# Delta-attention loop on one core: a loop turn takes two sequences (four tiles) instead of one (two tiles)

## The reference, cut to what matters

```
qkvz = x @ W_in                                # x is layer-normalised; 128 -> 4*1024
q, k, v = silu(conv4(q, k, v))                 # causal, 4 taps, per channel
q = l2norm(q) * HD ** -0.5 ; k = l2norm(k)
def step(S, (q, k, v, g, beta)):               # over the 256 tokens of a sequence, S starts at 0
    S = S * exp(g)
    S = S + k (outer) (v - k @ S) * beta
    return S, q @ S
y = y * rsqrt(mean(y*y) + 1e-6) * norm_w * silu(z)
x = x + y @ W_o
```

## Time and profile before

| | |
|---|---|
| median of 3 runs | 7055.97 us |
| lowest, highest | 7048.7, 7073.78 us |
| the profiled execution's own time | 7079.48 us |
| its span, first to last instruction | 7077.4 us |
| mean granted TensorE clock | 0.917 |
| PE busy over the span | 6006.2 us (85%) |
| DVE, ACT, POOL busy over the span | 3698.0, 3271.5, 2513.9 us |

### The profile page before, as it was taken

One profiled execution on the slowest core, in us unless ns is written; L12 is line 12 of the kernel. 1 busy time (PEld: TensorE's weight loads), 2 busy tenths in 40 slices (PEclk: granted clock), 3 DMA queues, 4 the chain that ended last, 5 costly groups with the idle time before them and its releaser, 6 DMA issues. The chain is left out here.

```text
span 7077.4 us, 188914 instructions
## 1 busy us (share of the span) xinstructions
PE 6006.2 (85%) x68003; PEld 4474.9 (63%) x68004; DVE 3698.0 (52%) x7183; ACT 3271.5 (46%) x7090; POOL 2513.9 (36%) x2357
## 2 busy tenths in 40 slices
PE   5999999999999999999999999675888678886587
PEld 4666666666666666666666666463666456665486
DVE  5555554555555554554555554654444456665433
ACT  2555554555555554554555554142333244553165
POOL 5445444444444444444444443342000100002554
PEclk9999998999999998999999999897999889997588
DMA  3000000000000000000000000111000000001124
GB/s 97 16 18 20 20 14 20 18 16 20 20 14 20 18 15 20 14 20 20 14 20 20 20 14 14 37 47 42 0 0 0 2 1 0 0 0 31 37 59 120
DMA packets 99093, 159.13 MB, mean 22 GB/s; under 512 B 19972, under 2 KB 82244, under 8 KB 96068
## 3 DMA queue, kind: packets, MB, share of 16 engines
q1 hardware_dynamic: 76260, 121.44, 5.3%
q0 software_dynamic: 14080, 26.64, 1.1%
q10 hardware_dynamic: 8320, 4.19, 0.2%
HBM read 118.03 MB, written 104.87 MB: 31 GB/s over the span
## 5 line engine op out<-in xcount | busy, mean ns | idle before, releaser
L784 PE MATMUL bank<-wc,hT 128*128 128x512 f32 x2088 | 1156.8, 676 | 120.9 <-issue 107.6
L941 PE MATMUL bank<-X,kqe 128*128 128x64 f32 x6240 | 774.2, 277 | 75.2 <-DVE rb L1426 54.6
L941 PEld LDWEIGHTS bank<-X,kqe 128*128 128x128 f32 x6240 | 726.3, 192 | 99.2 <-DVE rb L1426 70.2
L1171 ACT ACTIVATE TT<-bank 128x512 bf16<-128x512 f32 x640 | 382.1, 597 | 731.7 <-PE bank L922 729.3
L784 PEld LDWEIGHTS bank<-wc,hT 128*128 128x128 f32 x2088 | 393.0, 212 | 448.9 <-issue 425.8
L1465 DVE TENSOR_TENSOR yb<-bank,masks 128x512 bf16<-128x512 f32 x768 | 527.3, 687 | 256.4 <-PE bank L904 248.0
L1405 DVE TENSOR_TENSOR kqe<-bank,ex 128x512 f32<-128x512 f32 x520 | 335.1, 686 | 337.7 <-PE bank L850 337.7
L1301 POOL TENSOR_SCALAR_AFFINE_SELECT kqe<-kqe 128x512 f32<-128x512 f32 x260 | 215.0, 827 | 817.2 <-DVE kqe L1405 817.2
L1268 POOL TENSOR_TENSOR qa<-qa,qt 128x512 f32<-128x512 f32 x390 | 486.3, 1268 | 34.8 <-POOL qt L1263 34.8
L1171 ACT ACTIVATE T<-bank 128x512 bf16<-128x512 f32 x640 | 348.9, 595 | 272.6 <-PE bank L915 270.6
L1126 ACT ACTIVATE ex<-bank,gate_bias_all 128x128 f32<-128x128 f32 x1040 | 290.0, 372 | 384.6 <-DVE kqe L1405 183.6
(11 more groups left out here) (526 smaller groups left out, 13338.5 us busy)
## 6 DMA issues: line engine op xcount, KB each, us to landing
sent_l0f<-blank_l0f SPq DMA_DIRECT2D x64, 528.0 KB
sent_l1m<-blank_l1m SPq DMA_DIRECT2D x64, 528.0 KB
xin<-sent_l1m SPq DMA_DIRECT2D x139, 66.0 KB
taken_l1m<-back_l1m SPq DMA_DIRECT2D x16, 512.0 KB, 8.7
xin<-sent_l0f SPq DMA_DIRECT2D x75, 66.0 KB
decay_sums<-decay_rows SPq DMA_DIRECT2D x264, 3.0 KB
cw_stage<-in_L_attn_conv_w_dram SPq DMA_DIRECT2D x4, 1024.0 KB, 6.2
out_dram<-x_sb ACTq DMA_DIRECT2D x8, 512.0 KB, 6.8
```

Of the source, the lines that this page charges most:

```text
L784: mm = pe.matmul(bk[:, :], src[:, j:j + P], w["wc"][:, j, at * 512:(at + 1) * 512], start=(j == 0), stop=(j == TAPS - 1))
L941: mm = pe.matmul(bk[:, i * D0:(i + 1) * D0], lhsT(hh), rhs(hh), start=True, stop=True)
L1171: nc.scalar.activation(dst, bk[:, :].rearrange("p (h a u) -> p h a u", h=8, u=1 << l), ACT.Copy).then_inc(actb.done.sem, 1)
```

## The change

A turn now is `U = 2 * TPB = 4` slots: two whole sequences. There are 16 turns. All four slots are unrolled in each engine's loop, and what was bound to slot 0 or 1 goes by the slot's parity. Thresholds and indices that counted turns by two slots now count by four; signals that came once a turn (`kd_ready`, `rhs_ready`) come twice. SP's loop still issues one tile of blank rows and one set of decay rows in each slot. Buffers, ring sizes, the work in a slot and its order are as before. The diff, cut:

```diff
-    N = turns * TPB
+    U = 2 * TPB
+    N = turns * U
...
-            names += [f"tt.{l}.0", "s.0", f"tt.{l}.1", "s.1"] if l == 5 and t == 1 else [f"tt.{l}.0", f"tt.{l}.1"]
+            names += [f"tt.{l}.0", "s.0", f"tt.{l}.1", "s.1"] if l == 5 and t % 2 == 1 else [f"tt.{l}.0", f"tt.{l}.1"]
...
-        kd_ready = signal("kd_ready", 1)
-        rows_in = [signal(f"decay_rows_in{t}", 16 * NHB) for t in range(U)]
+        kd_ready = signal("kd_ready", U // 2)
+        rows_in = [signal(f"decay_rows_in{t}", 16 * NHB * U // TPB) for t in range(TPB)]
...
             with sp.Fori(0, turns) as b:
-                for t in range(TPB):
+                for t in range(U):
                     lone_wait(sp, actb.full.sem, actb.full.at(b, actb.uses.at(t - 1, "ex.3")), sp_passed)
-                    load(bass.ds(b * TPB + t + TPB, 1), t)
+                    load(bass.ds(b * U + t + TPB, 1), t % TPB)
                     for s in sendings:
-                        blank_tile(sp, s, bass.ds(b * TPB + t, 1))
+                        blank_tile(sp, s, bass.ds(b * U + t, 1))
...
             with pe.Fori(0, turns) as b:
-                for t in range(TPB):
-                    taps(b, hT[t], "v0", 2, 2)
+                for t in range(U):
+                    taps(b, hT[t % 2], "v0", 2, 2)
                     level_zero(b, t, 0)
...
-                                if t == 1:
+                                if t % 2 == 1:
                                     state(b, t, G)
...
             with act.Fori(0, turns) as b:
-                for t in range(TPB):
+                for t in range(U):
                     right_side(b, t)
...
             with pool.Fori(0, turns) as b:
-                for t in range(TPB):
+                for t in range(U):
...
             with dve.Fori(0, turns) as b:
-                for t in range(TPB):
+                for t in range(U):
...
-        delta_attention(nc, c, {"wc": wc, "wq": wq, "cq": cq, "wz": wz, "wo": wo}, x_all, mr, gates, decay_rows, tiles // TPB, sendings)
+        delta_attention(nc, c, {"wc": wc, "wq": wq, "cq": cq, "wz": wz, "wo": wo}, x_all, mr, gates, decay_rows, tiles // (2 * TPB), sendings)
```

More of the change, by code:

```diff
@@ L563, in at @@
     def at(self, t, name):
-        if t == TPB:
+        if t == len(self.slots):
             return self.ahead + self.per + self.behind.index(name) + 1
-        turn, slot = divmod(t, TPB)
+        turn, slot = divmod(t, len(self.slots))
         return self.ahead + turn * self.per + sum(map(len, self.slots[:slot])) + self.slots[slot].index(name) + 1
@@ L758, in _ @@
             with sp.Fori(0, turns) as b:
-                for t in range(TPB):
+                for t in range(U):
                     lone_wait(sp, actb.full.sem, actb.full.at(b, actb.uses.at(t - 1, "ex.3")), sp_passed)
-                    load(bass.ds(b * TPB + t + TPB, 1), t)
+                    load(bass.ds(b * U + t + TPB, 1), t % TPB)
                     for s in sendings:
-                        blank_tile(sp, s, bass.ds(b * TPB + t, 1))
+                        blank_tile(sp, s, bass.ds(b * U + t, 1))
             for t in range(TPB):
-                sp.wait_ge(rows_in[t].sem, 16 * NHB * (turns + 2))
+                sp.wait_ge(rows_in[t].sem, 16 * NHB * ((turns + 1) * U // TPB + 1))
             for s in sendings:
@@ L914, in join_t @@
                     hh = G * 8 + i
-                    mm = pe.matmul(bk[:, i * HALF:(i + 1) * HALF], TT[t][:, hh, :], yb[:, hh, :], start=True, stop=True)
+                    mm = pe.matmul(bk[:, i * HALF:(i + 1) * HALF], TT[t % 2][:, hh, :], yb[:, hh, :], start=True, stop=True)
                 mm.then_inc(actb.full.sem, 1)
@@ L1006, in _ @@
                     level_zero(b, t, 3)
-                    taps(b, hT[t], "v1", 0, 2)
+                    taps(b, hT[t % 2], "v1", 0, 2)
                     turn_zero(b, t, 2)
@@ L1031, in _ @@
                         if l <= 2:
-                            taps(b, hT[t], "v1", l + 1, 1)
+                            taps(b, hT[t % 2], "v1", l + 1, 1)
                         if l == 4:
@@ L1040, in _ @@
                     decayed(b, t)
-            b, t = turns - 1, TPB
+            b, t = turns - 1, U
             taps(b, hT[0], "v0", 2, 2)
@@ L1111, in squares_o @@
                     act.wait_ge(dveb.full.sem, dveb.full.at(b, 1))
-                elif t < TPB:
+                elif t < U:
                     dveb.was_full(act, b, t, "sq")
@@ L1201, in _ @@
                             if l < LEVELS - 1:
-                                columns(b, f"tt.{l}.{G}", group(TT[t], G), l, right)
+                                columns(b, f"tt.{l}.{G}", group(TT[t % 2], G), l, right)
                             else:
                                 bk = actb.empty(act, b, f"tt.{l}.{G}")
-                                nc.scalar.activation(group(TT[t], G)[0:HALF, :, HALF:],
+                                nc.scalar.activation(group(TT[t % 2], G)[0:HALF, :, HALF:],
                                                      bk[0:HALF, :].rearrange("p (h u) -> p h u", u=HALF), ACT.Copy
                                                      ).then_inc(actb.done.sem, 1)
-                            if l == 5 and t == 1:
+                            if l == 5 and t % 2 == 1:
                                 bk = actb.empty(act, b, f"s.{G}")
@@ L1237, in _ @@
             for zero in (hT[0][:, 0:TAPS - 1], x_all[:, N + 1:N + 3, :], hTz, mr[:, :, N:N + 2],
-                         gates["bias"][:, N, :], gates["dec"][:, turns, :]):
+                         gates["bias"][:, N, :], gates["dec"][:, N // TPB, :]):
                 pool.memset(zero, 0.0)
@@ L1325, in _ @@
                     lone_wait(pool, proj.full.sem, proj.full.at(b, proj.uses.at(t, "z1")), pool_passed)
-                    pool.tensor_copy(hTz, hT[t][:, TAPS - 1:]).then_inc(kept_ready.sem, 1)
+                    pool.tensor_copy(hTz, hT[t % 2][:, TAPS - 1:]).then_inc(kept_ready.sem, 1)
                     decayed(b, t)
-            b, t = turns - 1, TPB
+            b, t = turns - 1, U
             gate_o(b, t)
@@ L1484, in _ @@
                             scale_k(b, t)
-                    if t == 1:
-                        E = bass.ds(b, 1)
+                    if t % 2 == 1:
+                        E = bass.ds(b * (U // 2) + t // 2, 1)
                         for half in range(2):
```

27 lines of the change are left out of this document (13 added, 14 removed).

## The result

The changed kernel takes 6931.81 us in the median of four runs (6929.66 to 6940.05), the kernel before 7058.95 (7048.70 to 7073.78, four runs, three of them those shown ahead of the prediction). The ratio is 0.982, with a 95% interval of 0.9801 to 0.984: 127 us faster. The forecast was 6985 us, with 6936 to 7022 as its range. The direction was right and the size was not: it is 4 us outside the range, and the gain is 1.8 times the 71 us of the sum. (Three executions in the later groups, two of the kernel before and one of u32, ran far slower, at a granted clock of 0.54 to 0.74; the ratios leave them out, the medians don't.)

A forecast was written before the change was run, and what follows sets the result against it. PE bounds the delta loop and waits most at the loop branch; 16 of 31 taken branches go at 4.46 us each (gap 3.47, clock 0.99), 71 us, all else 0: 7055.97 - 71 = 6985 us, range 6936 to 7022.

The forecast's parts named there:

- the 71 us of the sum: Delta loop on PE: 16 removed branches at 4.46 us each, gap and clock together; all other terms at 0.
- What bounds the loop: Delta loop: PE is the bound, busy 3927.32 of 4277.67 us; its largest wait is at the branch.
- The gap of 3.47 us, 16 times: PE's idle "issue" wait at each taken branch ahead of line 784, taken as a mean over 31; 16 go.
- The clock, 0.99 us a branch: PE's half-clock running behind a branch: 0.99 of the 4.46 us between mean and first even slot.
- the 59 to 61 us that were named as the sign: Time that even slots without a branch would take if the forecast was right.
- The ends of the range: Gain bounds from the shortest and longest even slots behind a branch: 45 us (16 x 2.80) and 120 us (16 x 7.50).
- Nothing late at the new passage: Passage from slot 1 to slot 2: other engines are on time without the gap, ACT with 1.49 us in hand; 0 us.
- The other engines' code: Longer loop bodies may be fetched again each turn; hidden, 0 us. As rival: stops inside slots, 7173 us, chance 0.06.
- Both signs that were named for this rival: Queue 14 blocks between 283 and 4400 us, and "issue" waits on ACT or DVE, would show the code-fetch rival.
- The median: Whole kernel: the 71 us taken off the three-run median 7055.97 us, 23.5 us below the profiled execution; gives 6985 us.

The follow-up runs named there:

- u32: The changed kernel with 32 slots a turn, 2 turns, instead of four slots; 6930.80 us, ratio 0.9807 to the kernel before.
- pe_long: The changed kernel with four slots a turn on PE only; ACT, DVE, POOL and SP keep two; 6943.98 us, ratio 0.9818.
- pe_short: The changed kernel with PE's loop back at two slots a turn, ACT, DVE, POOL and SP at four; 7068.84 us, ratio 1.0025.
- idle: The changed kernel with PE waiting at the end of slot 1 for three extra DVE reductions; 7150.72 us, ratio 1.0085.
- work: The changed kernel with slot 1's output projection done three times instead of once, keeping PE busy; 7039.86 us.
- before_again: The kernel before, unaltered, measured and traced once more; 7102.75 us, ratio 1.0021.
- after_again: The changed kernel, unaltered, measured and traced once more; 6986.84 us, ratio 0.9853 to the kernel before.
- u8: The changed kernel with eight slots a turn, 8 turns, instead of four slots; 6925.51 us, ratio 0.9801 to the kernel before.
- after_c: The changed kernel, unaltered, measured again in the third group; 6983.26 us, ratio 0.9857 to the kernel before.
- u32_c: The changed kernel with 32 slots a turn, measured again in the third group beside after_c; 6951.95 us, ratio 0.9801.

## Why the prediction was wrong, step by step

- *What bounds the loop*: right. PE alone, and within PE the branch. pe_long and pe_short show it from both sides.
- *The gap of 3.47 us, 16 times*: the sum is right, and in part by luck. 55.5 us were expected and idle time on PE fell by 55.4. But the prediction took the mean, seeing "no reason that they are the dear or the cheap ones", and the 16 gaps that went are the cheap ones, 2.81 us each in the trace of before. They are worth 44.9 us. The 15 that remain became 16.0 us shorter, which the prediction excluded ("The 15 branches that remain cost what they cost now"): 12 of them are now of the short kind of about 2.8 us. With 5.5 us more of other waits, the two errors cancel.
- *The clock, 0.99 us a branch*: this is the step that failed. It is the difference between the mean even slot and the first one, "the first even slot is entered by falling into the loop, without a branch, and takes 59.77 us". I took that slot as what an even slot costs without a branch. Its row says 0.97: it had a half-clock stretch of its own, and the slots without a branch take 58.24, under the 59 to 61 us that were named as the sign. (The split was a little off too: by the busy times of the earlier trace rows, 1.22 of the 4.46 us are the clock and 3.24 idle time.) By place 2 alone a branch cost 63.66 - 58.24 = 5.42 us, of which 2.90 is idle time and 2.53 the clock, where the sum had 0.99. The half clock was also less in slots that the branch doesn't touch: over the loop the clock gave 60.8 us where the sum had 16 x 0.99 = 16. The experiment idle shows why that is no accident: a pause of 3.9 us on PE costs 7.99 us in the slot behind it and some more in the others; work shows that the same time spent busy does not.
- *The ends of the range*: I had 120 us as the outer end and called it one, because the longest slots hold half-clock stretches "that no branch made". The experiment idle shows that a pause costs half-clock time outside its own slot as well (9 to 15 us in each of the other places), so that was the wrong reason to leave it out of the likely case.
- *Nothing late at the new passage*: right, ACT's 1.49 us of slack is there.
- *The other engines' code*: right in the price. Both signs that were named for this rival came, 186 blocks of queue 14 in the loop and 53.2 us of "issue" waits on ACT, and its price did not: ACT stops at the 15 remaining branches alone, not in the middle of a slot, and PE's own gap there hides it, as the sum had it. The rule of the Trainium skill ("Runtime: NRT & Kernel Launch", section "Instruction fetch mechanics"), that the engines other than PE hold 512 instructions, foretold this stop of ACT, whose body is 643: the trace agrees, with waits of up to 4.3 us at the branch, and DVE (443) and POOL (271) have none. Whose code the blocks are no view says. They are 12.4 a turn, against 7 in the earlier trace rows, when bodies half as long came in; that suggests that more than ACT's was fetched, but it is not shown.
- *The median*: the profiled execution of before was 23.5 us above the median, and I took that off the forecast as it stood. Part of such differences lies behind the loop, in a stage with two levels (below): of the 149.8 us between the two first profiled executions, 116.2 are the loop and 33.9 the stretch behind it. In the two other groups that measured the changed kernel the medians are 105 and 116 us apart, with ratios of 0.9853 and 0.9857. By these ratios 7056 us would have become 6952 or 6955, inside the range. So whether the time falls 4 us outside it or not is a matter of the group. That the clock was mis-sized is not: the loop lost 116 and 131 us in the two pairs of traces (before and after, before_again and after_again), where the sum has 71.

What stays open: which slots inside a turn fall to the half clock, why place 1 got slower (22.9 us) when place 3 got faster, and why the gaps that remain became shorter. The experiments show that idle time on PE brings the half clock and busy time doesn't; they don't explain the pattern.

## What to carry to other kernels

Where TensorE bounds a stage, count a pause of 1.5 to 4 us on it at about twice its length or more, as in this kernel, and look first at the pauses, not at the products: here 32 waits of 1.5 us, filled with products that were there anyway, gave 83 us of the loop (2.6 us each), and 16 branches taken out gave 116 (7.3 each). To price what a piece costs, take the base from a stretch whose clock is 1.00, not from the first one that happens to lack the piece. Unrolling a loop pays as long as branches are many; here from one branch in 132 us to one in 264 it paid 1.5 to 1.8%, and beyond that hardly anything before the other waits were filled.

## What the runs showed of the hardware that was not expected

- The pause that a branch brings on PE comes in two kinds, about 2.8 and about 4.2 us. Before, they took turns; the changed kernel has mostly short ones (46.7 us in 15 times). With eight slots a turn five of the seven lie between the kinds (3.4 to 3.8 us) and two are longer, 4.9 and 6.1 (28.4 us in 7 times). What sets the length was not tried.
- POOL stops at the branch only where its body is long: never with 137 or 271 instructions (before, the changed kernel), and 7 times in u8, 36.6 us together, where the body is some 540 (an estimate from 137 and 271).
- The second routing stage (line 2275, 16 groups) has two levels within the same program: 12.6 us a group in one execution, 14.6 in another, all groups of an execution nearly alike. In the longer one ACT starts about 2 us after the products that it needs have ended. The view of that line, first trace of the changed kernel and then after_again:

```profile
  PE bank L2249: 50.0, 16
```

```profile
  PE bank L2229: 53.8, 10
  remote: 27.2, 5
  PE bank L2249: 3.2, 1
```

  It is 32 us of a run, and goes by the execution: the traces of two groups of runs had 14.6 throughout (14.7 in the third group), those of the second 12.6. What sets it was not tried.
- The first routing stage takes from 164 to 205 us, from its first to its last product with `before_l0f` on PE, though its code is the same: 164 us in the first trace of either kernel and in after_c, 171 in after_again, 203 in u32 and 202 in u32_c, 205 in pe_long. In u32_c it has the lower clock shown above.
